# Ten units instead of nine for the softmax row maxima of a fused attention and expert kernel

## The reference

```
xn = layernorm(x)
s  = attention with weights 1 - tanh(energy)^2 (causal), normalised, times V, times Wo
h  = rmsnorm(xn) * norm1_w
X1 = xn + (softmax(q k^T / sqrt(8)) v) wo          # 16 heads, 512 x 512 scores, no mask
g  = silu(X1 + shared expert + top-2 of 8 experts of rmsnorm(X1) * norm2_w)
out = x + s * g
```

## Time and profile before

| | us |
|---|---|
| median of 3 runs | 1172.72 (1171.72 to 1175.66) |
| the profiled execution | 1171.43 |
| its span, first to last instruction | 1169.6 |
| PE busy | 1055.8 (90%) |
| DVE busy | 839.3 (72%) |
| ACT busy | 648.9 (55%) |
| POOL busy | 340.6 (29%) |

### The profile page before, as it was taken

The page is one execution under the profiler, slowest core; times in us unless marked ns, Lnnn a source line. Parts: engine busy times, 40 slices in busy tenths (PEclk is TensorE's granted clock), DMA queues, the critical chain, the costliest instruction groups (busy, mean ns, idle before and its releaser), DMA issues.

```text
span 1169.6 us, 18848 instructions
## 1 busy us (share of the span) xinstructions
PE 1055.8 (90%) x7112; PEld 487.0 (42%) x7112; DVE 839.3 (72%) x1692; ACT 648.9 (55%) x873; POOL 340.6 (29%) x178
## 2 busy tenths in 40 slices
PE   3469999899999899999999999989999999999998
PEld 1112465224651356424553246523464235532465
DVE  7366887659767687677876598765976868764872
ACT  4038842597227972388524983269722786248822
POOL 6500354005430335203351045301542033510023
PEclk9559999999998999999998999999999999989999
DMA  5530244104420045202350034400442012610020
GB/s 176 108 59 2 63 117 70 29 2 88 126 37 28 22 76 130 52 2 50 83 118 28 3 73 111 66 28 3 95 122 41 21 40 58 143 29 1 2 73 10
DMA packets 71787, 69.68 MB, mean 60 GB/s; under 512 B 8528, under 2 KB 63056, under 8 KB 71568
## 3 DMA queue, kind: packets, MB, share of 16 engines
q1 hardware_dynamic: 68928, 64.41, 25.0%
q10 hardware_dynamic: 2768, 4.06, 1.0%
HBM read 53.37 MB, written 14.81 MB: 58 GB/s over the span
## 4 chain that ended last, share of the span: by engine, by line
PE 66%; ACT 13%; DVE 12%; issue 4%; DMA 2%; SPq 2%; POOL 1%; ACTq 0%; POOLq 0%; DVEq 0%
PE O L977 12%; PE O L993 10%; ACT PT L534 7%; PE S L1009 6%; DVE PT L685 6%; PE M L919 6%; PE S L1011 6%; PE S L1010 6%; PE S L952 6%; PE M L916 5%; DVE nmax L648 3%; PE M L902 2%; ACT L534 2%; PE M L1082 2%; PE M L908 1%
## 5 line engine op out<-in xcount | busy, mean ns | idle before, releaser
L534 ACT ACTIVATE PT<-S 128x1024 f32<-128x1024 f32 (+1 forms) x448 | 420.0, 972 | 100.7 <-PE S L952 98.9
L648 DVE TENSOR_REDUCE nmax<-M 128x1 f32<-128x512 f32 x512 | 332.8, 685 | 121.1 <-PE M L916 75.5
L685 DVE SCALAR_TENSOR_TENSOR PT<-PT 128x768 f32<-128x768 f32 (+1 forms) x192 | 215.6, 1170 | 95.6 <-ACT PT L534 95.2
L977 PE MATMUL O<-PT,V 128*12 128x256 f32 (+3 forms) x2816 | 251.1, 438 | 0.0
L409 POOL TENSOR_TENSOR split<-split,parts 128x512 f32<-128x512 f32 x32 | 91.1, 2846 | 463.3 <-ACT parts L495 463.3
L952 PE MATMUL S<-stackQ,stackK 64*128 64x512 bf16 (+3 forms) x1024 | 202.1, 356 | 21.3 <-DMA stackQ<-mTZ 7.3
L568 ACT ACTIVATE PT<-S 128x1024 f32<-128x1024 f32 x72 | 73.9, 1027 | 257.9 <-PE S L1011 257.8
L424 POOL TENSOR_TENSOR PT<-PT,CB 128x1024 f32<-128x1024 f32 x56 | 133.3, 2387 | 283.7 <-DMA CB<-scrC 175.0
L1009 PE MATMUL S<-h2hi,wgu_hi 128*128 128x512 f32 x288 | 151.4, 526 | 0.0
L993 PE MATMUL O<-PT,wdn 128*128 128x512 f32 x288 | 142.8, 595 | 0.0
L916 PE MATMUL M<-KX,stackQ 128*128 128x512 bf16 x256 | 105.6, 414 | 26.0 <-DMA KX<-scrK 22.8
(11 more groups left out here) (177 smaller groups left out, 1034.8 us busy)
## 6 DMA issues: line engine op xcount, KB each, us to landing
CB<-scrC SPq DMA_DIRECT2D x64, 256.0 KB, 5.4
stackQ<-scrQ SPq DMA_DIRECT2D x192, 64.0 KB
stackK<-scrK SPq DMA_DIRECT2D x192, 64.0 KB
scrQ<-parts SPq DMA_DIRECT2D x16, 384.0 KB, 4.5
scrK<-parts SPq DMA_DIRECT2D x16, 384.0 KB, 8.7
KX<-scrK SPq DMA_DIRECT2D x96, 32.0 KB
PT<-in_w_gu ACTq DMA_DIRECT2D x2, 1152.0 KB, 7.8
xin<-in_x SPq DMA_DIRECT2D x8, 256.0 KB, 3.0
```

The source lines that it names most:

```text
L534: a.activation(PT[:, n % SLOTS, 2 * q * w:2 * q * w + 2 * w].rearrange("p (r n) -> p r n", r=2), S[k][:, :].rearrange("p (r n) -> p r n", ...
L648: v.tensor_reduce(nmax[:, h % 2, h // 2, t:t + 1], M[k][:, :], AX.X, ALU.max, negate=True).then_inc(m_read[k], 1)
L685: v.scalar_tensor_tensor(p, p, 1.0, p, ALU.subtract, ALU.mult).then_inc(weighed, 1)
L977: last = t_.matmul(O[k][32 * q:32 * q + VW, i0:i1], V[:, j, 4 * g + q, :], PT[:, n % SLOTS, w * q + at:w * q + at + i1 - i0], start=(j == ...
```

## The change

The 32 maxima of Y and Z stand in units 0 to 9 and no longer in units 0 to 8, and the counts are evener. Unit 0 had 1 and has 3, units 1 and 2 had 4 and have 3, unit 3 keeps 4, unit 4 had 4 and has 3, unit 5 keeps 3 (and `maxT_Y` as the third of its four names), units 6 and 7 had 4 and have 3, unit 8 keeps 4, unit 9 had none and has 3. Y now ends with the last maximum of unit 4 and Z begins in unit 5. `maxT_Z` moves from unit 9 to unit 10, and DVE's split of Z from behind unit 8 to behind unit 9.

```diff
-spread(MAX["Y"], {0: 1, 1: 4, 2: 4, 3: 4, 4: 3})
-spread(MAX["Z"], {4: 1, 5: 3, 6: 4, 7: 4, 8: 4})
+spread(MAX["Y"], {0: 3, 1: 3, 2: 3, 3: 4, 4: 3})
+spread(MAX["Z"], {5: 3, 6: 3, 7: 3, 8: 4, 9: 3})
 PLACES[5].insert(2, "maxT_Y")
-PLACES[9] += ["maxT_Z"]
+PLACES[10] += ["maxT_Z"]
...
                     if n == 4:
                         maxima_parts(u, "Y")
-                    if n == 8:
+                    if n == 9:
                         maxima_parts(u, "Z")
```

## The result

The changed kernel takes 1213.09 us (median of 4 runs, 1210.74 to 1214.16) beside 1173.81 for the kernel before in the same comparison: 1.0332 times as long, 95% interval 1.0306 to 1.0359. The profiled execution has a span of 1212.4 us, 42.8 more than before.

A forecast was written before the change was run, and what follows sets the result against it. Bound: first-stage maxima, then a fixed hand-over barely covered by ACT. 1171.43 + 14.4 (late mTZ) + 13.6 (clock fall) = 1199.4, said as 1200 us; own range 1193 to 1208, whole range 1181 to 1212 with 6 us of low stretches.

The forecast's parts named there:

- What bounds the kernel: First stage: maxima up to mTZ, then a fixed hand-over of 4.1 to 4.3 us, covered by ACT's stock within 0.2 us.
- that rival's margin: Y's transfer before unit 8: 0.4 us to spare; without it at most 0.5 us more per row, 1204 us, chance 0.08.
- Start and units 0 to 9: Unit 3's first scores 0.46 us earlier, unit 10's 1.29 earlier; maxima relieved by about 1 us per batch row.
- the walk: Unit-by-unit timing of the batch row from 902.48: mTZ 1.59 us later, at 931.65 instead of 930.06.
- The rival of a free maximum: Maxima beside scores cost PE nothing; units of three take 1.82 us, deciding below 2.02: 1163 us, chance 0.06.
- PE's pause and its clock: Ahead of unit 12 the pause grows from 1.03 to about 3.6 us, the clock falls: 1.7 us per row, 13.6 us.
- Rows with a longer low clock: Three of eight batch rows 2.0 us late, three 1.6, two 1.8: 14.4 us; shifting low stretches up to 6 us either way.

The follow-up runs named there:

- the two halves: Against the kernel before: only Y's new counts, 1178.31 us (1.0058); only Z evened to three a unit through unit 9, turned in unit 10, 1212.95 us (1.0366).
- the turning one unit earlier: Changed kernel with maxT_Z moved from unit 10 to the end of unit 9, counts of maxima kept: 1186.3 us, 1.0139 of the kernel before.

## Why the prediction was wrong in size

*What bounds the kernel* held: the hand-over of 4.1 us, its cover on ACT, and the move of mTZ behind that cover. One line of the change causes most of the loss (the two halves; the turning one unit earlier). PE has no wait for the transfer of Y in the profile, so that rival's margin was there.

*Start and units 0 to 9.* I had mTZ 2.0 us late in rows with the long low stretch and 1.6 in the others. Measured: 29.27 to 29.36 us after the load before in the three long rows, 31.46 to 31.75 in the seven after, 2.35 late; at full clock 2.0 late. Eight times 2.35 are 18.8 us where I had 14.4. Two parts of the walk failed. Unit 5 took 2.96 us and not 2.69: with Y ending in the last maximum of unit 4, DVE's split stands right behind the reduction that it needs (before, one of Z lay between), later reductions slip by 0.2 us, and the turning of Y waits 0.30. And the 0.46 us by unit 3 were hardly there: I let unit 2's product follow bare scores, but the last maximum of unit 1 stands right ahead of them, and at the half clock the two take 511.60 - 510.64 = 0.96 us together. In rows at full clock the lead by unit 3 is 0.15 us. The pace of units of three held: 534.23 - 531.98 = 2.25 us, 2.29 predicted.

*The rival of a free maximum* fell with that: 2.25 us is above its 2.02. In the timeline above a maximum (531.97) and a score half (531.98) start together, but beside it the pair of halves takes 0.60 us, where a bare pair takes 0.39: the half that uses the maximum's rows starts some 0.2 us behind the other. The Trainium skill, TensorEngine Tiling (Array Packing), section "Key Properties", says that different tiles can run matmuls in parallel; the trace agrees for the maximum and the half on other rows, and the 0.2 us are the half on its own rows.

*PE's pause and its clock.* 3.5 us (3.6 predicted), and the clock fell behind it in all eight batch rows. A low step is 1.52 us and not 1.41: the ratio came from steps with two maxima, and what these add grew only from 1.20 - 0.87 = 0.33 us to 1.94 - 1.52 = 0.42, while the bare step grew by three quarters. Hand-over and units 12 to 15 cost 16.9 us in the profile, one late transfer of 1.05 included; 13.6 predicted. The Trainium skill, TensorE: Matmul & The Clock Gate, section "HAM oscillation — how this bites in real kernels", agrees with these rows: the wait for a transfer throttled PE anew in every round.

*Rows with a longer low clock* is the step that failed. I took the mix of the starts' low stretches as unchanged and gave them up to 6 us either way. They all went one way: what is left of the 25.2 us up to mTZ beside 18.8 is 6.4 us. It was no chance: a longer row alone, with no maximum moved, brought mTZ 5.8 us later in sum. (Each mix is that of one profiled execution.) I had treated a thing that depends on the length of the row, which I predicted to change by 28.0 / 8 = 3.5 us, as noise about zero. So 18.8 + 6.4 + 16.9 = 42.1 us stand where I had 14.4 + 0 + 13.6 = 28.0, each term short on the same side, and the range of 1181 to 1212, built on one term missing at a time, ended 1 us too low; its upper ends together, 1208 and 6 us, would have reached 1214. Why rows some 143.3 us apart keep the long stretch, and why rows some 140 us apart do so in the run with the turning one unit earlier, stays open.

## What to carry to other kernels

A hand-over of fixed length is paid for by the work queued behind its first step: before moving that step later in an in-order queue, count what moves from behind it to ahead of it. Where a wait grows on the engine that is the bound, price its clock too, and take a clock state that depends on the period of the loop as a term with a sign, not as scatter. Idle time of PE ahead of dense work can be worth filling with products that nobody reads: 14 us of 1171 here.

## What the runs showed of the hardware

The clock at a row's start reacts to small pauses: four added matmuls in a pause of 0.88 us left three of seven rows without a low stretch, three more in the next pause of 0.64 us all seven. Low stretches in the stages came in lengths of 3.4, 6.8 and 10.2 us; at the start the shortest costs 1.3 us of stage time (39.06 to 40.3), the longest some 1.6 us more (42.0). In the kernel before, a lone pause of 0.9 to 1.0 us ahead of unit 12, or of 1.3 us in the second stage, did not take the clock down in any of the seven rows that another row follows; 3.5 us in the changed kernel did each time.
